# Cross attention's scores in three fp32r products of parts, the parts made 1.5 batches ahead, and the transfer queue ordered by a batch's last weights

## The reference

```python
kv_r   = rope(ctx)                                    # 64 x 257 x 128
scores = einsum('bhsr,bhlr->bhsl', q_r, k_r)          # 16 heads, 32 queries, 257 keys
attn   = softmax(scores, axis=-1)
ctx_c  = einsum('bhsl,bld->bhsd', attn, kv_r)
out    = x + project(ctx_c)                           # w_vo: 16 heads x 128 -> 512
```

## Time and profile before

| | |
|---|---|
| median of 3 runs | 1698.99 us (1696.46 to 1701.09) |
| the profiled execution | 1701.08 us, its span 1699.3 us |
| busy over the span | PE 88%, PEld 66%, DVE 66%, ACT 48%, POOL 32% |
| mean granted TensorE clock | 0.947 |
| cross attention's scores | first at 474.4 us, last at about 960 us |
| in the steady part of that stage (600 to 900 us) | PE 96 to 97%, DVE 80%, ACT 54%, POOL 49 to 51%, clock 1.00 |

### The profile page before, as it was taken

The page is one execution under the profiler, slowest core; times in us unless marked ns, Lnnn a source line. Parts: engine busy times, 40 slices in busy tenths (PEclk is TensorE's granted clock), DMA queues, the critical chain, the costliest instruction groups (busy, mean ns, idle before and its releaser), DMA issues. The chain is left out here.

```text
span 1699.3 us, 26369 instructions
## 1 busy us (share of the span) xinstructions
PE 1490.1 (88%) x8136; PEld 1129.8 (66%) x8136; DVE 1126.8 (66%) x1816; ACT 809.9 (48%) x1723; POOL 540.8 (32%) x594
## 2 busy tenths in 40 slices
PE   5799999999758999999999929997689499999996
PEld 3577777777546777777777728886234277777775
DVE  6788877887346877877887625775628626464746
ACT  4556656556434555555555414554100344545553
POOL 4234433331034455455445312120321311312202
PEclk9899999999978999999999969998889699999998
DMA  4132333432366444454444122000253000000000
GB/s 155 54 106 85 115 99 106 124 105 87 91 205 197 121 118 115 108 124 109 108 123 114 43 103 93 0 0 1 84 237 149 0 1 1 26 1 25 1 25 25
DMA packets 138010, 143.77 MB, mean 85 GB/s; under 512 B 83169, under 2 KB 102753, under 8 KB 134241
## 3 DMA queue, kind: packets, MB, share of 16 engines
q1 hardware_dynamic: 136224, 133.86, 27.0%
q10 hardware_dynamic: 1728, 9.20, 1.6%
HBM read 113.54 MB, written 29.49 MB: 84 GB/s over the span
## 5 line engine op out<-in xcount | busy, mean ns | idle before, releaser
L901 ACT ACTIVATE c_e_t_high<-c_et_ps 128x512 fp32r<-128x512 f32 x128 | 76.7, 599 | 227.1 <-PE c_et_ps L966 227.1
L794 POOL TENSOR_TENSOR c_mixed_low<-c_whole,c_mixed_high 128x512 fp32r<-128x512 f32 x64 | 95.3, 1489 | 174.8 <-ACT c_mixed_high L913 174.8
L77 DVE TENSOR_TENSOR b_rot_parts_low<-b_rot,b_rot_parts_high 128x1536 fp32r<-128x1536 f32 x64 | 135.8, 2122 | 21.8 <-ACT b_rot_parts_high L526 21.8
L958 PE MATMUL c_sc_ps<-c_kv_t,c_q 128*128 128x257 f32 x512 | 136.3, 390 | 15.1 <-DMA c_q<-carried_queries 15.1
L1518 PE MATMUL f_ps<-f_right,f_left 128*128 128x512 f32 x256 | 115.3, 612 | 27.7 <-DMA f_right<-ent_out 20.4
L817 DVE TENSOR_REDUCE c_peak<-c_sc_ps 128x2 f32<-128x514 f32 x128 | 88.5, 692 | 56.7 <-PE c_sc_ps L958 56.0
L264 POOL TENSOR_TENSOR b_turned_raw<-b_turn_part 128x384 f32<-128x384 f32 x32 | 70.0, 2188 | 167.6 <-DVE b_key_parts_low L77 166.3
L70 PE MATMUL e_mm_ps<-folded_high,e_h_t_high 128*128 128x512 f32 x256 | 108.8, 425 | 15.8 <-DVE e_h_t_low L77 15.6
L958 PEld LDWEIGHTS c_sc_ps<-c_kv_t,c_q 128*128 128x128 f32 x512 | 99.1, 195 | 34.2 <-DMA c_q<-carried_queries 15.9
L309 DVE TENSOR_TENSOR b_rot<-b_w_qr,b_angle 128x1536 f32<-128x1536 f32 x64 | 119.1, 1861 | 0.2
L893 ACT ACTIVATE c_e<-c_sc_ps,c_peak 128x257 f32<-128x257 f32 x256 | 118.8, 475 | 0.0
(11 more groups left out here) (212 smaller groups left out, 3956.5 us busy)
## 6 DMA issues: line engine op xcount, KB each, us to landing
c_q<-carried_queries SPq DMA_DIRECT2D x64, 256.0 KB, 3.7
c_ends_spread<-end_weights SPq DMA_DIRECT2D x64, 256.0 KB, 4.3
carried_queries<-x SPq DMA_DIRECT2D x7, 2048.0 KB, 11.2
b_early<-early SPq DMA_DIRECT2D x15, 640.0 KB, 4.0
c_raw<-cache_t SPq DMA_DIRECT2D x64, 128.5 KB, 3.9
c_swapped<-cache_t SPq DMA_DIRECT2D x128, 64.2 KB, 3.9
f_left<-ent_in SPq DMA_DIRECT2D x8, 1024.0 KB, 5.3
f_right<-ent_out SPq DMA_DIRECT2D x8, 1024.0 KB, 8.0
```

What stands on the lines that cost most here:

```text
L77: return nc.vector.tensor_tensor(low, value, high.bitcast(F32), ALU.subtract)
L794: nc.gpsimd.tensor_tensor(mixed[1][:, w, :, u], whole[:, u % 2].rearrange("p (h s) -> p h s", h=H), mixed[0][:, w, :, u].bitcast(F32), ALU ...
L958: last = nc.tensor.matmul(sc_ps[:, 2 * half + c, 0:L], q[:, u, at], kv_t[:, u], start=True, stop=True)
```

## The change

The scores are no longer a plain f32 product. ACT rounds the rotated context (now 258 columns, the last one zero) into `keys[0]` and the query into `q_parts[0]`; DVE makes the low part of the keys (`split_keys`), POOL that of the query (`split_query`). All of this is done for batch b+2 in the odd step of batch b, but for POOL's part, which is done for batch b+1 in the even step of b. PE then makes six fp32r matmuls of 258 columns for a pair in place of two f32 ones of 257. The query buffers go from four to two. SP's order is written anew: for batch b it stores the last key's weights, loads the query of b+3, spreads the weights, and loads the context of b+6.

```diff
-        q = sb("c_q", [P, BT, H * S])
+        q = sb("c_q", [P, 2, H * S])
+        q_parts = pair("c_q_parts", [P, 2, H * S])
+        keys = pair("c_keys", [P, 2, LE])
...
                 for u in range(BT):
                     b = BT * i + u
...
+                    store_ends(b, u % 2)
...
+                        load_query(b + 3, (u + 1) % 2)
+                    spread_ends(b, i, u)
+                    if not (last and b + 6 >= B):
+                        load_context(b + 6, (u + 2) % BT)
...
+            sp.wait_ge(crossing.staged_out, 16 * (H // 2 - 1))
+            sp.wait_ge(crossing.last_out[0], 16)
+            for b in range(3):
+                load_query(b, b % 2)
+            for b in (BT, BT + 1):
+                load_context(b, b - BT)
             in_tiles(sp, tile)
...
+            def split_query(b, v):
+                pool.wait_ge(q_rounded, b + 1)
+                nc.gpsimd.tensor_tensor(q_parts[1][:, v], q[:, v], q_parts[0][:, v].bitcast(F32), ALU.subtract).then_inc(q_split, 1)
...
                     keep_ends(n, i, u, half)
+                    if half == 0 and not (isinstance(b, int) and b + 1 >= B):
+                        split_query(b + 1, (u + 1) % 2)
...
+            def split_keys(b, u):
+                dve.wait_ge(keys_rounded, b + 1)
+                low_part(nc, keys[1][:, u % 2], kv_t[:, u], keys[0][:, u % 2]).then_inc(keys_split, 1)
...
                     if half == 0:
                         split_kv(b, u)
+                    elif not (isinstance(b, int) and b + 2 >= B):
+                        split_keys(b + 2, (u + 2) % BT)
...
+            def round_scoring(b, t, u):
+
+                act.wait_ge(rotated_, b + 1)
...
+                wait(act, scored, 2 * (b - 2) + 2)
+                nc.scalar.activation(keys[0][:, u % 2], kv_t[:, u], ACT.Copy).then_inc(keys_rounded, 1)
+                act.wait_ge(q_loaded[u % 2], 32 * t + 16 * (u // 2) + 16)
+                nc.scalar.activation(q_parts[0][:, u % 2], q[:, u % 2], ACT.Copy).then_inc(q_rounded, 1)
...
                         round_mixed(b - 1, (u - 1) % BT, i if u else i - 1, w if u else 1 - w)
+                    if half == 1 and not (isinstance(b, int) and b + 2 >= B):
+                        round_scoring(b + 2, i + (u + 2) // BT, (u + 2) % BT)
...
                 if half == 0:
-                    pe.wait_ge(q_loaded[u], 16 * (t + 1))
-                    pe.wait_ge(rotated_, b + 1)
+                    pe.wait_ge(q_split, b + 1)
+                    pe.wait_ge(keys_split, b + 1)
...
-                    last = nc.tensor.matmul(sc_ps[:, 2 * half + c, 0:L], q[:, u, at], kv_t[:, u], start=True, stop=True)
+                    last = multiply_parts(nc, sc_ps[:, 2 * half + c, 0:LE], [a[:, u % 2, at] for a in q_parts],
+                                          [a[:, u % 2] for a in keys], True, True)
```

More of the change, by code:

```diff
@@ L706, in cross_attention @@
         x_loaded = sem("c_x_loaded")
-        q_loaded = [sem(f"c_q_loaded{u}") for u in range(BT)]
+        q_loaded = [sem(f"c_q_loaded{v}") for v in range(2)]
+        keys_rounded, keys_split, q_rounded, q_split, padded = (
+            sem(f"c_{n}") for n in ("keys_rounded", "keys_split", "q_rounded", "q_split", "padded"))
         rotated_, kv_turned, kv_rounded, kv_split, pool_chained = (
@@ L736, in _, with load_query, load_context, store_ends @@
         def _(sp):
[L737 to L740, removed]
+            def load_query(b, v):
+                wait(sp, q_split, b - 1)
+                sp.dma_start(q[:, v], q_in[bass.ds(b, 1)].rearrange("b d x -> d (b x)")).then_inc(q_loaded[v], 16)
+            def load_context(b, u):
+                sp.wait_ge(rotated_, b - BT + 1)
+                crossing.load(sp, b, u)
+            def store_ends(b, v):
                 sp.wait_ge(ended, 2 * b + 2)
-                sp.dma_start(ends_dram[at].rearrange("b p c -> p (b c)"), ends[:, v]).then_inc(ends_stored[v], 16)
+                sp.dma_start(ends_dram[bass.ds(b, 1)].rearrange("b p c -> p (b c)"), ends[:, v]).then_inc(ends_stored[v], 16)
+            def spread_ends(b, i, u):
+                v = u % 2
                 sp.wait_ge(ends_stored[v], 32 * i + 16 * (u // 2) + 16)
-                sp.dma_start(ends_spread[:, v], ends_dram[at].rearrange("b p c -> b (p c)").to_broadcast([P, P * CH])).then_inc(ends_back[v], 16)
+                sp.dma_start(ends_spread[:, v], ends_dram[bass.ds(b, 1)].rearrange("b p c -> b (p c)").to_broadcast([P, P * CH])).then_inc(ends_back[v], 16)
             def tile(i, w):
@@ L748, in tile @@
                     b = BT * i + u
[L749 to L761, removed]
+                    last = isinstance(b, int)
+                    store_ends(b, u % 2)
+                    if not (last and b + 3 >= B):
+                        if last and b + 3 == BT:
+                            sp.wait_ge(crossing.last_out[1], 16)
+                            sp.wait_ge(crossing.last_out[2], 16)
+                        load_query(b + 3, (u + 1) % 2)
+                    spread_ends(b, i, u)
+                    if not (last and b + 6 >= B):
+                        load_context(b + 6, (u + 2) % BT)
                 sp.dma_start(x1[:, bass.ds(i, 1)].rearrange("p t d -> p (t d)"),
                              x_tiles[bass.ds(i, 1)].rearrange("t p d -> p (t d)")).then_inc(x_loaded, 16)
+            sp.wait_ge(crossing.staged_out, 16 * (H // 2 - 1))
[4 more added lines that the diff above has]
+                load_context(b, b - BT)
             in_tiles(sp, tile)
-            for u in range(BT):
-                spread_ends(TILES - 1, u)
             sp.wait_ge(x_loaded, 16 * TILES)
@@ L778, in rotate @@
                 pool.wait_ge(pool_chained, 2 * b + 2)
-                wait(pool, scored, 2 * (b - BT) + 2)
                 wait(pool, kv_turned, b - BT + 1)
                 wait(pool, mix_taken, b - BT + 1)
-                nc.gpsimd.tensor_tensor(kv_t[:, u], part[:, 0], part[:, 1], ALU.add).then_inc(rotated_, 1)
+                nc.gpsimd.tensor_tensor(kv_t[:, u, 0:L], part[:, 0], part[:, 1], ALU.add).then_inc(rotated_, 1)
                 pool.wait_ge(rotated_, b + 1)
+            def split_query(b, v):
+                pool.wait_ge(q_rounded, b + 1)
+                nc.gpsimd.tensor_tensor(q_parts[1][:, v], q[:, v], q_parts[0][:, v].bitcast(F32), ALU.subtract).then_inc(q_split, 1)
             def keep_ends(n, i, u, half):
@@ L876, in tile @@
                         keep_moments(i - 2)
+            split_keys(0, 0)
             find_peak(0, 0)
             normalise(0, 0)
+            split_keys(1, 1)
             in_tiles(dve, tile)
@@ L902, in round_turned @@
                                      ACT.Copy).then_inc(et_rounded, 1)
+            def round_scoring(b, t, u):
+                act.wait_ge(rotated_, b + 1)
+                if isinstance(b, int) and b == 0:
+                    act.wait_ge(padded, 1)
+                wait(act, scored, 2 * (b - 2) + 2)
+                nc.scalar.activation(keys[0][:, u % 2], kv_t[:, u], ACT.Copy).then_inc(keys_rounded, 1)
+                act.wait_ge(q_loaded[u % 2], 32 * t + 16 * (u // 2) + 16)
+                nc.scalar.activation(q_parts[0][:, u % 2], q[:, u % 2], ACT.Copy).then_inc(q_rounded, 1)
             def round_kv(b, u):
```

7 lines of the change are left out of this document (6 added, 1 removed).

## The result

The changed kernel takes 1822.95 us, the median of 4 runs (1821.85 to 1825.70), beside 1699.70 for the kernel before on the same chip (1696.46 to 1701.09): a ratio of 1.073, with a 95% interval of 1.0711 to 1.075. It is slower, as forecast, but by 123 us and not by 55.

The account below looks back on a forecast made before the run. PE was taken to bound odd steps, the division even ones. DVE's new instruction adds 0.90 us to 62 batches (55.8), the start 2, the queue -3: 54.8 on 1701.1, so a median of 1754 us, range 1738 to 1771.

Parts of the forecast that it names:

- What bounds the kernel: Odd steps (3.45 us) are PE's without a gap; in even steps PE waits for DVE's division.
- The score block at 0.70 us: Six fp32r products on PE take 0.70 us in place of 0.87, saving 0.17 where PE is the limit.
- rival 2: Six score products take 1.38 us, as the skill's weight-load rule would suggest; even steps reach 4.10, total 1769; 5 in 100.
- The wait of DVE for ACT's keys: In the odd step DVE stands still 0.75 us before `split_keys`, until ACT has rounded the keys.
- rival 1: The wait on ACT costs nothing, odd steps lose 0.17 us, total about 1688; 4 in 100.
- It starts 0.03 after ACT's end and takes 0.42: `split_keys` on DVE in the odd step, timed by earlier rows, ends at 707.15; the step becomes 4.35 us.
- "Free" for POOL's query part: POOL's low part of the query, 1.46 us in the even step, delays nobody until it took 2.5 us.
- "unchanged" for the even step: Even steps stay at 3.77 us, 4.54 with `add_out`, the score block still ending before the division.
- The start: At the stage's start, rounding the first query and making its low part delay the first product by 2 us.
- The queue: SP's new order brings back 3 of at most 10.6 us in the first six batches, otherwise without effect.
- Rival 3: PE's idle time lowers its clock for the whole stage, total about 2065; 2 in 100.
- The direction: The whole kernel becomes slower by over 0.3%: 94 in 100; faster 4, same 2.

Follow-up runs that it names:

- the last experiment: Kernel before the change, with only the division moved ahead of `split_kv` and `add_out` in DVE's even step: 1680.44 us, ratio 0.9879.
- the two kernels whose odd step is PE's again: Changed kernel with `split_keys` behind the odd step's division: 1734.98 us; with it in DVE's even-step gap, POOL's rotation and ACT's roundings also moved: 1693.61 us.
- the first experiment: Changed kernel with POOL's low part of the mixed result cut from 16 heads to one: 1773.28 us (one run).
- the third experiment: Changed kernel with POOL's low part of the query cut from 512 columns to 32: 1802.65 us (one run).

## Why the prediction was half right

- **What bounds the kernel**: right. PE's in the odd step, the division's in the even one; the last experiment takes the latter wait away, and PE is busy 99.6 of 100.
- **The score block at 0.70 us**: right. The products follow each other 0.11 and 0.12 us apart (774.15, 774.26, 774.38). This refutes rival 2, and for these products the Trainium skill's rule on weight loads that the prediction sets behind it: each of them has its own weight load on the whole array. The 0.17 us saved appears as 3.45 to 3.28 in the two kernels whose odd step is PE's again.
- **The wait of DVE for ACT's keys**: right in place and near in size, 0.87 us where 0.75 stood; rival 1 fell on it.
- **"It starts 0.03 after ACT's end and takes 0.42"**: this is the step that failed. The start was right (0.03); the length was 1.30. The row used, the context's low part in the earlier trace rows, has one input in PSUM. `split_keys` has both in SBUF, and POOL's `split_mixed`, which runs in the odd step too, began 0.26 us ahead of it. The term of the wait was 0.90 a batch; the hold adds 0.87, by the first experiment some 50 us of the 69 that were missing (1822.95 - 1754). The step put the instruction on ACT's and DVE's timeline and did not lay POOL's beside it.
- **"Free" for POOL's query part, and "unchanged" for the even step**: wrong by 0.33 us a batch, 20 us by the third experiment. I had asked when PE and ACT need POOL's results, and they get them in time; I had not asked which DVE instruction POOL's would lie on.
- **The start**: +2 became -0.15. The first product is 1.62 us late, but the 1.28 us of ACT's table load, which stood behind the first scores before (the row below), now begin at 474.61 beside the query's low part; and the first pair's scores are 0.41 us faster (476.06 to 477.76, where DVE looks for their maximum, against 474.44 to 476.55). **The queue**: -3 was given for a cause that is worth nothing alone; against the 12.6 us due, the first six batches came out 6 us cheaper.
- **Rival 3**: refuted, the granted clock is 1.00 from 700 to 800 us with PE busy 74 of 100.
- **The direction**: "slower" came true by the forecast's own wait of 0.90 us a batch, so it was not luck. The size was wrong by the two terms on POOL.

The table load in the kernel before, from the timeline of the stage's start:

```profile
477.35 1.28 ACT L893 ACT_TABLE_LOAD   x1 [16.90 <-DVE c_peak L817]
```

The trace of before had the hold in it, in both orders. The same POOL instruction takes 1265 to 1783 ns there, and I read its 1.46 us as its length: it began beside the odd step's division and ended 1.14 us after it (706.80, 707.94). The even step's division ended 0.54 us after POOL's rotation (703.61, 703.07); it was lengthened by no more than 0.02 there, but in other steps of that kernel it takes up to 0.87 us. From that kernel's timeline, and its own row of POOL's instruction:

```profile
702.43 0.64 POOL L782 TENSOR_TENSOR c_kv_t<-c_part 128x257 f32<-128x257 f32 x1 [0.32 <-POOL c_part L777]
...
702.90 0.71 DVE L824 TENSOR_TENSOR c_e<-c_e,c_inverse 128x512 f32<-128x512 f32 x1
```

```profile
L794 POOL TENSOR_TENSOR c_mixed_low<-c_whole,c_mixed_high x64: 1265/1460/1783, 497.8 to 971.6; 128x512 fp32r<-128x512 f32 x64
```

A spread of 0.5 us in an elementwise instruction of one shape was the sign to ask what it meets.

## What to carry to other kernels

Before pricing a new DVE instruction by a row of the same size, look at where its inputs lie, and lay POOL's timeline over the place: with both inputs in SBUF, and POOL's instruction begun first, its end was POOL's end plus its own columns. In the same way, work given to POOL is only free if no DVE instruction of that kind falls under it, or under the POOL instructions that it pushes back. When PE is 97% busy and still waits for one instruction in every other step, moving that instruction up was worth 1.2% here, and shortening PE's work 0.4% at best.

## What the hardware showed that I had not expected

An instruction of DVE with two SBUF inputs that began while POOL's was running ended 0.27 to 0.30 us after POOL's with 258 columns, 0.53 to 0.56 with 512 where it was lengthened, and 0.02 with two; that is the time of its columns at 1.06 ns each, so it seems to do nothing until POOL is through. In the other order POOL's instruction is the long one, 1.41 to 1.72 us for 1.27. Whatever its length, it ended 1.12 to 1.15 us after the division did, in 40 steps of the kernel before and 42 of the last one (600 to 900 us). DVE's context part, with one input in PSUM, took its 0.42 from 773.85, while POOL's `rotate` ran from 773.54 to 774.18 (all from the changed kernel's timeline).

The Trainium skill's page "SBUF — State Buffer", in the section "SBUF: two separate sides", states the rule: DVE and GpSimd share a pair of ports under an exclusive lock; a DVE instruction with two SBUF inputs and a GpSimd instruction that reads SBUF take it from each other, the first to start has it for its whole length and the other blocks fully. The runs agree, in both orders and with the numbers above, but for the fixed part of the blocked instruction, 0.13 to 0.15 us, which seems to pass while it is blocked. Read for this change, that rule would have made `split_keys` wait for the end of POOL's 1.27 us.

ACT's table load, 1.28 us, began in the changed kernel while the exponentials that need it were still waiting for the first scores, and so cost the start nothing.
